# A Mamba, adapter and expert kernel: half of the scanned states leave PSUM through ScalarE and are summed by accumulating turns on TensorE, and the loop over blocks is written out

## What is computed

```
xz = hidden @ in_proj_w.T;  x, z = split(xz)              # 1024 channels each
xc = silu(causal conv over 4 tokens of x)
dt_r, Bc, Cc = split(xc @ x_proj_w.T)                     # 128, 16 and 16 columns
delta = softplus(dt_r @ dt_proj_w.T + dt_proj_bias)
def step(h, inp):                                         # h: 1024 channels x 16 states
    delta_t, B_t, C_t, x_t = inp
    dA = jnp.exp(delta_t[..., None] * A)
    h = h * dA + (delta_t * x_t)[..., None] * B_t[:, None, :]
    y_t = jnp.einsum('bdn,bn->bd', h, C_t)                # sum over the 16 states
    return (h, y_t)
y = (y + xc * D_param) * silu(z);  out = y @ out_proj_w.T
```

## Time and profile before

| what | value |
|---|---|
| median of 3 runs | 2280.05 us (2276.32 to 2281.9) |
| the profiled execution's own time | 2278.81 us |
| its span in the profile | 2276.7 us, mean granted TensorE clock 0.886 |
| busy over the span | PE 1808.2 (79%), PEld 1315.3 (58%), DVE 1619.5 (71%), ACT 791.7 (35%), POOL 1060.2 (47%) us |
| Mamba stage in the profile | scans from 132.0 to 1255.5 us, four blocks, each 283.3 us from one block's first scan to the next (699.00 to 982.28) |
| after it | adapter and expert stages up to the end |

### The profile page before, as it was taken

The page is one execution under the profiler, slowest core; times in us unless marked ns, Lnnn a source line. Parts: engine busy times, 40 slices in busy tenths (PEclk is TensorE's granted clock), DMA queues, the critical chain, the costliest instruction groups (busy, mean ns, idle before and its releaser), DMA issues. The chain is left out here.

```text
span 2276.7 us, 31205 instructions
## 1 busy us (share of the span) xinstructions
PE 1808.2 (79%) x8084; PEld 1315.3 (58%) x8084; DVE 1619.5 (71%) x2168; ACT 791.7 (35%) x1172; POOL 1060.2 (47%) x793
## 2 busy tenths in 40 slices
PE   3778767687676875768857659799988999999988
PEld 3345434454344543445534336577877888888887
DVE  0379989999899998999989354355735555555554
ACT  0444555445554445544455012210002222222222
POOL 1157557676576755767557050000005444444443
PEclk9988889788797978978879779899998999999999
DMA  5112111121011210112101142311025655565653
GB/s 137 61 33 72 38 28 34 39 72 38 28 34 39 72 40 26 34 42 69 42 24 38 61 159 81 134 56 56 21 84 115 152 134 122 145 149 115 149 143 65
DMA packets 81603, 169.61 MB, mean 74 GB/s; under 512 B 22459, under 2 KB 27467, under 8 KB 77979
## 3 DMA queue, kind: packets, MB, share of 16 engines
q1 hardware_dynamic: 57360, 116.06, 15.6%
q0 software_dynamic: 17856, 44.85, 10.2%
q10 hardware_dynamic: 6187, 6.37, 1.1%
HBM read 261.62 MB, written 39.24 MB: 132 GB/s over the span
## 5 line engine op out<-in xcount | busy, mean ns | idle before, releaser
L789 POOL TENSOR_TENSOR dbx<-u,b_all 128x512 f32<-128x512 f32 x512 | 641.5, 1276 | 354.8 <-DVE h L687 349.8
L687 DVE TENSOR_TENSOR_SCAN h<-da,dbx 128x512 f32<-128x512 f32 x512 | 596.1, 1202 | 44.5 <-ACT da L587 44.5
L587 ACT ACTIVATE da<-delta,a_neg 128x504 f32<-128x504 f32 x512 | 347.8, 684 | 469.7 <-DVE h L687 460.7
L427 PE MATMUL hT<-ident,h 128*128 128x128 f32 x2048 | 314.3, 313 | 224.5 <-DVE h L687 224.1
L427 PEld LDWEIGHTS hT<-ident,h 128*128 128x128 f32 x2048 | 274.9, 163 | 338.0 <-issue 331.3
L700 DVE SCALAR_TENSOR_TENSOR yacc<-hT,c_now,yacc 128x512 f32<-128x512 f32 x480 | 331.1, 731 | 4.3 <-PE hT L427 4.2
L334 PE MATMUL bank<-hid,w_in 128*128 128x512 f32 x608 | 290.7, 626 | 7.6 <-ACT hid L467 7.6
L1919 POOL DMA_INDIRECT out<-y,slots_kept x76 | 140.1, 1844 | 132.0 <-DMA slots_kept<-lists_kept 60.6
L334 PEld LDWEIGHTS bank<-hid,w_in 128*128 128x128 f32 x608 | 120.6, 208 | 136.3 <-issue 127.6
L1554 POOL DMA_DIRECT2D slots_kept<-lists_kept x1 | 0.6, 577 | 335.5 <-DVE lists_kept L1508 335.5
L1906 POOL DMA_INDIRECT xg_kept<-x_scratch,slots_kept x72 | 71.2, 988 | 173.8 <-issue 170.0
(11 more groups left out here) (235 smaller groups left out, 3413.5 us busy)
## 6 DMA issues: line engine op xcount, KB each, us to landing
w_up_kept<-in_up_T SPq DMA_DIRECT2D x76, 1408.0 KB, 6.2
w_dn_kept<-in_dn_T SPq DMA_DIRECT2D x76, 768.0 KB, 7.5
b_all<-bt_scratch SPq DMA_DIRECT2D x128, 256.0 KB, 3.2
x_in<-in_x_pad ACTq DMA_DIRECT2D x21, 256.0 KB
res<-in_x_pad SPq DMA_DIRECT2D x20, 256.0 KB, 3.5
x_scratch<-res SPq DMA_DIRECT2D x20, 256.0 KB, 3.4
w_in<-in_in_T SPq DMA_DIRECT2D x8, 512.0 KB, 5.0
x_in<-x_scratch SPq DMA_DIRECT2D x4, 1024.0 KB, 5.3
```

The lines of the kernel that those rows point to most:

```text
L427: mm = nc.tensor.transpose(hT[t][:, d * P:(d + 1) * P], h[:, m % RING, d, t * P:(t + 1) * P], ident[:])
L587: nc.scalar.activation(out[:, :, 1:], rows[:, :, 1:], ACT.Exp, scale=a_neg[:, d, n:n + 1]) \
L687: nc.vector.tensor_tensor_scan(h[:, n % RING, i, :], da[i % RING][:], dbx[:, i, :], 0.0, ALU.mult, ALU.add).then_inc(scan_done, 1)
L789: nc.gpsimd.tensor_tensor(dbx[:, i, :], u[:, d, :], b_all[:, m % RING, :], ALU.mult) \
```

## The change

The token tiles of a step are split between two ways. Tiles 2 and 3 (t >= BY_ACT) go on as before, through VectorE, but share one PSUM tile `hT_dve`. Tiles 0 and 1 are turned into one PSUM tile `hT_act`; ScalarE writes C times it to SBUF (`scaled`, into `hc`), and TensorE turns `hc` back with 4 transposes that accumulate in two PSUM banks `ysum` over the 16 states (`sum_up`). The four banks of hT before make room for `hT_act`, `hT_dve` and the two of `ysum`. The turn of `yacc` has half the transposes (2 uses instead of 4), VectorE adds `ysum` to `skip` apart (`add_summed`), and the gates of half 1 are two of twice the width (`gate_half`). The loop over the blocks becomes Python's, so that each engine's code is written out four times.

The order on the engines moves too. `turn_h` is now called for one tile at a time, in the order 2, 0, 1, 3. `sum_up` of tile 1 runs one step later. `first_of(m)` names the piece that stands in the middle of the step, behind the turns of tiles 2 and 0, and the rest of the pieces stand at its end. ScalarE's `scaled` stands behind decay 2 of the next step (tile 0) and behind decay 0 of the step after that (tile 1). VectorE has one `add_state` behind scan 1 and one behind scan 3 (in the first step of a half behind scan 0 and scan 1).

```diff
+def first_of(m):
+    mine = [piece for piece in LINE[m] if name_and_number(piece)[0] in EMPTIED_BY_ACT | EMPTIED_BY_DVE - {"turn"}]
+    return mine[:1] if m % NST < NST - 1 else []
...
     da = [ps(f"da{i}", [P, BLK]) for i in range(RING)]
-    hT = [ps(f"hT{t}", [P, HT * P]) for t in range(TB)]
+    hT_act = ps("hT_act", [P, HT * P])
+    hT_dve = ps("hT_dve", [P, HT * P])
+    ysum = [ps(f"ysum{q}", [P, 2, BY_ACT * P]) for q in range(PAIRS)]
...
+            def turn_h(M, t):
+                pe.wait_ge(scan_done, SCAN0 + HT * (M + 1))
+                if t < BY_ACT:
+                    pe.wait_ge(hc_made, BY_ACT * M + t)
+                    bank, full = hT_act, hT_act_full
+                else:
+                    pe.wait_ge(sum_done, BY_DVE * M + t - BY_ACT)
+                    bank, full = hT_dve, hT_dve_full
+                for d in range(HT):
+                    mm = nc.tensor.transpose(bank[:, d * P:(d + 1) * P], h[:, M % RING, d, t * P:(t + 1) * P], ident[:])
+                mm.then_inc(full, 1)
+
+            def sum_up(M, t):
+                n = M % NST
+                pe.wait_ge(hc_made, BY_ACT * M + t + 1)
...
+                for d in range(HT):
+                    mm = nc.tensor.matmul(ysum[d // 2][:, d % 2, t * P:(t + 1) * P], hc[:, t, d * P:(d + 1) * P], ident[:],
+                                          start=(n == 0 and t == 0 and d % 2 == 0), stop=(n == NST - 1), is_transpose=True, skip_group_check=True)
+                mm.then_inc(ysum_step, 1)
...
-            with pe.Fori(0, NBLK) as j:
+            for j in range(NBLK):
                 for m in range(STEPS):
-                    for piece in mine[:1]:
+                    first = first_of(m)
+                    if n == 0:
+                        piece_of("body", j, mine.pop(0))
+                    turn_h(M, 2)
+                    turn_h(M, 0)
+                    if n == 1:
+                        sum_up(M - 1, 0)
+                    if M:
+                        sum_up(M - 1, 1)
+                    for piece in first:
                         piece_of("body", j, piece)
-                    turn_h(j, m, range(0, TB // 2))
-                    for piece in mine[1:]:
+                    turn_h(M, 1)
+                    turn_h(M, 3)
+                    if n:
+                        sum_up(M, 0)
+                    for piece in mine[len(first):]:
                         piece_of("body", j, piece)
-                    turn_h(j, m, range(TB // 2, TB))
...
+            def scaled(M, t):
+                act.wait_ge(hT_act_full, BY_ACT * M + t + 1)
+                if M:
+                    act.wait_ge(ysum_step, BY_ACT * (M - 1) + t + 1)
...
+                nc.scalar.mul(hc[:, t, :], hT_act[:], c_all[:, j % RING, t, n:n + 1]).then_inc(hc_made, 1)
...
                     for i in range(HT):
                         decay(j, *divmod(m, NST), i)
+                        if i == 0 and M >= 2:
+                            scaled(M - 2, 1)
+                        if i == 2 and M:
+                            scaled(M - 1, 0)
                         if m and i % RING == RING - 1:
                             mine = [piece for piece in LINE[m - 1] if name_and_number(piece)[0] not in EMPTIED_BY_DVE | {"gate"}]
-                            for piece in (mine[:1] if i == RING - 1 else mine[1:]):
+                            first = [piece for piece in mine if piece in first_of(m - 1)]
+                            for piece in (first if i == RING - 1 else [piece for piece in mine if piece not in first]):
                                 piece_of("body", j, piece)
```

More of the change, by code:

```diff
@@ L37 @@
 SCANS = STEPS * HT
-SUMS = STEPS * TB
+ALL_STEPS = NBLK * STEPS
 RING = 2
+PAIRS = HT // 2
+BY_ACT = 2
+BY_DVE = TB - BY_ACT
 BESIDE = [
@@ L100, in uses_of @@
         of[piece] = []
-        for _ in range(HT if name == "turn" else 1):
+        for _ in range(PAIRS if name == "turn" else 1):
             uses.append(Use(uses, name in EMPTIED_BY_ACT))
@@ L243, in mamba, with c_ready @@
     x1_rows = x1_d.rearrange("(k t p) f -> k t p f", t=TB, p=P)
+    def c_ready(j):
+        return (Place("body", j - 1, "ct") if j else Place("ahead", 0, "ct")).dve + 1
     with nc.Block() as block:
@@ L374, in dt_proj, with turn @@
                     .then_inc(bank_full, 1)
-            def turn(at, half):
-                pe.wait_ge(sum_done, at.block * SUMS + SUM0 + (0 if half else SUMS // HALVES))
-                for d in range(HT):
-                    bank = take(at, d)
-                    for t in range(TB):
-                        mm = nc.tensor.transpose(bank[:, t * P:(t + 1) * P], yacc[:, t, d * P:(d + 1) * P], ident[:])
+            def turn(at, M):
+                pe.wait_ge(sum_done, BY_DVE * M)
+                for q in range(PAIRS):
+                    bank = take(at, q)
+                    for i in range(2):
+                        for t in range(BY_DVE):
+                            d = 2 * q + i
+                            mm = nc.tensor.transpose(bank[:, (i * BY_DVE + t) * P:(i * BY_DVE + t + 1) * P],
+                                                     yacc[:, t, d * P:(d + 1) * P], ident[:])
                     mm.then_inc(bank_full, 1)
@@ L647, in make_u, with add_turned, add_summed, gate_half @@
                 nc.vector.tensor_tensor(u[:, d, :], delta[:, d, :], xc[:, d, :], ALU.mult).then_inc(u_ready, 1)
[L649 to L654 removed]
+            def add_turned(at, half, q):
+                d = half * HT + 2 * q
+                dve.wait_ge(skip_ready, at.block * DT + (0 if half else d + 2) + SKIP0)
+                dve.wait_ge(bank_full, at.full + q + 1)
+                mine = skip[:, d:d + 2, BY_ACT * P:]
+                nc.vector.tensor_tensor(mine, banks[at.uses[q].bank][:].rearrange("p (i c) -> p i c", i=2), mine, ALU.add) \
+                    .then_inc(dve_emptied, 1)
+            def add_summed(M, half, q):
+                d = half * HT + 2 * q
+                dve.wait_ge(ysum_step, BY_ACT * M)
+                mine = skip[:, d:d + 2, 0:BY_ACT * P]
+                nc.vector.tensor_tensor(mine, ysum[q][:], mine, ALU.add).then_inc(ysum_out, 1)
+            def gate_half(at, M, q):
+                d = HT + 2 * q
+                dve.wait_ge(zs_ready, at.block + Z0)
+                dve.wait_ge(dve_emptied, at.dve + q + 1)
+                dve.wait_ge(ysum_out, PAIRS * (M // NST - 1) + q + 1 if M else 0)
+                nc.vector.tensor_tensor(skip[:, d:d + 2, :], skip[:, d:d + 2, :], zs[:, d:d + 2, :], ALU.mult) \
+                    .then_inc(y_ready[1], 2)
+            def finish_half(section, j, M):
+                half = 0 if M % STEPS else 1
+                at = Place(section, j, f"turn{half}")
+                if M:
+                    for q in range(PAIRS):
+                        add_summed(M, half, q)
                 if half:
[L657 to L659 removed]
+                    for q in range(PAIRS):
+                        gate_half(at, M, q)
             def residual(at, j, t):
@@ L745, in _ @@
                                 make_u(Place("body", j, piece), name_and_number(piece)[1])
-                    if n == NST - 1:
-                        for t in range(TB):
-                            add_state(j, g, n, t)
                 for piece in LINE[STEPS - 2]:
@@ L751, in _ @@
                         make_u(Place("body", j, piece), name_and_number(piece)[1])
-            for i in range(HT):
-                add_skip(Place("after", NBLK, "turn1"), 1, i)
+            for t in range(BY_DVE):
+                add_state(ALL_STEPS - 1, t)
+            for q in range(PAIRS):
+                add_turned(Place("after", NBLK, "turn1"), 1, q)
+            finish_half("after", NBLK, ALL_STEPS)
             for piece in AFTER:
@@ L803, in _ @@
                 piece_of("ahead", 0, piece)
-            with pool.Fori(0, NBLK) as j:
+            for j in range(NBLK):
                 for m in range(STEPS):
```

117 lines of the change are left out of this document (63 added, 54 removed).

## The result

The kernel after the change takes 2663.3 us (median of 4 runs, 2659.4 to 2669.4) against 2278.2 us for the kernel before (median of 4, 2275.8 to 2281.9). The ratio is 1.169, 95% interval 1.166 to 1.172: it is 17% slower, 17 us under the forecast of 2680. The profiled execution took 2662.8 us and spans 2661.0.

The account below looks back on a forecast made before the run. VectorE was taken to bound the kernel before. Steps lengthened by waits add 72 us a block, 288 in all, to 2278.8, giving 2567; the clock's 112 makes the forecast 2680 us, range 2530 to 2810.

Parts of the forecast that it names:

- x steps: Steps whose first TensorE piece is x, with two ScalarE operations: 10.7 us at full clock against 9.38 before.
- The loop through D: D: end of a step's last `add_state`; TensorE's turns and first piece wait for it; z step 10.0 us against 7.1.
- Odd out steps: Steps 6, 8, 10, 12: VectorE's residual waits for the out piece behind D; 12.4 us against 8.3.
- Even out: Steps 5, 7, 9, 11: tile 3's turn behind an unread piece; 6.95 us, 11.3 in 7 and 11, 9.2 in 9.
- The late pieces: Other pieces in ten steps, behind `sum_up` of tile 0: 2.2 to 2.8 us each, or 4 to 4.4.
- silu: Step 22, ScalarE's table loads and activations: waiting of 7.5 us after the change, 5.72 before.
- Added work: Per block: 64 `scaled` on ScalarE, 42 us; accumulating transposes on TensorE, 31 us; no engine full by its own work.
- VectorE's loss of work: Two `add_state` fewer a step on VectorE: 42 us a block, 166 us over four blocks.
- The clock: TensorE's clock stays at mean 0.84, now in VectorE's path: +28 us a block, +112 in all; chance 0.60.
- The loop written out: Python loop over blocks: removes 2 to 3 us of idle time at a block's start, nothing more.
- The first rival: TensorE's clock stays full because turns fill what were gaps: 2567 us; chance 0.12.
- the second: TensorE's clock low for most of the stage, mean 0.70: +62 us a block, 2815 us; chance 0.15.

Follow-up runs that it names:

- experiment 2: Kernel after, with each step's first piece ahead of its turns again and the others in the middle: 2206.2 us, ratio 0.973 to the kernel before.
- 3: Kernel after, with ScalarE emptying the first piece's bank behind decay 3 of the next step instead of decay 1: 2479.4 us.
- 4: Kernel before, with the first piece behind the turns of tiles 0 and 1, the others at the step's end: 2443.9 us.
- experiment 5: Kernel after, with only the first pieces ahead of their turns again, the other pieces left at the step's end: 2348.2 us.
- Experiment 7: Kernel after, with three of `sum_up`'s four transposes left out from the second state on: 2664.0 us.
- experiment 10: The kernel of experiment 2, with the convolution ahead of the second `add_state` of its step: 2219.1 us.
- 8: Kernel after, with the turns of tiles 1 and 3 issued twice: 2704.2 us.
- 9: Kernel after, with the turns of tiles 1 and 3 issued three times: 2835.3 us.
- experiment 1: Kernel before, with only the loop over the four blocks written out on all five engines: 2265.4 us, ratio 0.998.
- 6: The kernel of experiment 2, with odd out pieces one step earlier and silu in ScalarE's place behind decay 1: 2210.7 us, ratio 0.971.
- 11: The kernel of experiment 2, with three of `sum_up`'s four transposes left out for every state but the first: 2205.4 us.

## Why the prediction was right

The forecast held by its mechanism, and the time came within 17 us of it. Block 3 takes 382.2 us from its first scan (887.71) to the next block's (1269.94); the sum said 355 at the full clock and 28 for the clock, 383. By the same cuts:

| part of a block | forecast, clock at full | measured |
|---|---|---|
| steps 1 to 12 | 134 | 143.4 |
| steps 13 to 20 | 90 | 99.0 |
| steps 21 to 30 | 108 | 116.4 |
| boundary | 23 | 23.5 |
| clock | 28 | in the three above: 9.4 + 9.0 + 8.4 = 26.8 |

The last line is only what the measured parts have above the sum at the full clock. It holds the clock's part together with the errors of the single terms, and these have both signs: z and x steps at the full clock took 0.6 to 0.8 us less than was put, step 9 took 5.0 us more and step 13 4.7 us more. No run separates them, so it is in part luck that 26.8 and 28 agree.

- **The loop through D.** Shown by the z step above and by experiments 2, 3 and 4: moving the pieces back gives 457 us, moving the reader 184, moving only the pieces in the kernel before costs 173. The z step was put at 10.0 and took 9.37 at the full clock. Two terms were too large. The first is 0.25 us until ScalarE starts, 0.04 by the rows. The second is decay 2, `scaled`, decay 3 and scan 3 in a row: scan 3 stands behind scan 2, not behind decay 3, so from the end of the copy to the last `add_state` it is one decay and two scans. From decay 2 (936.37) to the next D (940.06) that is 3.69 us where 3.9 was put. The shown step is the quickest of the four z steps; together with the late dt4 and dt5 they took 47.95 us (905.76 to 953.71) where 40.4 + 5.6 = 46.0 was put, at a clock between 0.83 and 1.00.
- **x steps** were put at 10.7 at the full clock and took 9.95, for the same two terms. Where the clock was low they took longer. The rows show three D in a row, since the convolution starts at D. The first of the two steps between them begins at the half clock, the second is at the full one:

```profile
1115.40 2.96 DVE L694 SCALAR_TENSOR_TENSOR xc<-xpad,ch,xc 128x512 f32<-128x512 f32 x3
...
1128.17 2.96 DVE L694 SCALAR_TENSOR_TENSOR xc<-xpad,ch,xc 128x512 f32<-128x512 f32 x3
...
1138.12 2.96 DVE L694 SCALAR_TENSOR_TENSOR xc<-xpad,ch,xc 128x512 f32<-128x512 f32 x3
```

  The first step took 12.77 us and the second 9.95. The piece took 5.16 us in the first (1118.22, clock rising within it) and 3.60 in the next, and each of the three sets ahead of it 0.9 and 0.44.
- **Odd out steps** were put at 12.4, with a wait of about 5 us at the residual: 12.24 (960.81 to 973.05), with 5.19. **Even out**: step 5 was put at 6.95 and took 7.10. Steps 7 and 11 were put at 11.3 and took 12.9 and 12.8. Step 9 was put at 9.2 and took 14.2, at a mean clock of 0.61 and with a wait of 3.72 us of the `add_state` for its turn, which was not in the sum. The four even ones together were 47.0 in place of 38.8, the clock's part included: these steps are where the sum was furthest off.
- **The late pieces** were put at 2.2 to 2.8 or 4 to 4.4 us in ten steps, which the expectation of experiment 5 made 25 to 30 us a block; that experiment shows 142 / 4 = 35, the clock's part included.
- **silu** was put at 7.5 us of waiting, measured 7.72. The wait stands at another place than before: it is scan 0 of step 23 that waits for its decay (1164.54), since silu now stands behind decay 3 of step 22.
- **Added work.** A `scaled` 0.676 us (0.687 taken); a set of four accumulating transposes 0.60 as recorded, 0.43 from start to start (0.48 taken). Experiment 7 shows that the transposes did not make the time, and experiment 2 that all of the added work together did not.
- **VectorE's loss of work** was put at 166 us. The `add_state` lost 164 (349.1 to 184.7, both forms), but VectorE only 128: its operations that read two tensors in SBUF got slower (experiment 10 shows why). In the stage the convolutions grew from 73.7 to 88.6 us, `correct` from 22.9 to 30.4, `make_u` from 28.3 to 34.9. That cost was not in the sum; in the kernel after it is hidden by the waits, in experiment 2, where VectorE lost 138 us of work, it is part of why only 64 of the 166 us came back. The greater part is 65 us more of idle time.
- **The clock** was forecast to stay as it was: 0.84 in the stage, before and after. The first rival (full clock) and the second (0.70) both fall. What the 0.84 cost in us was taken from the share of TensorE in the path, and no run measured it. The Trainium skill's rule, TensorE: Matmul & The Clock Gate, Part 4 (PE-mode transpose), that transposes do not count as activity for the clock gate, is what stood behind the second. The runs contradict it for the fp32 transposes of this kernel: 18, 24, 32 and 40 transposes a step (experiment 7, the kernel after, 8 and 9) go with 0.77, 0.84, 0.89 and 0.89.
- **The loop written out** was to take 2 to 3 us at each block's start: experiment 1 shows 5 us less in all, with an interval from 9 less to 1 more, which can't be told from nothing.

Where the gain of experiment 2 stops is told from its groups: VectorE's work fell by 138 us in the stage and its idle time grew from 51 to 116. That its remaining waits can be removed was tried twice (6 and 11) without a gain; whether another order does it is open.

## What to carry to other kernels

When work is moved to another engine, follow the order of the instructions, not the shares of busy time: a producer placed behind something that waits for the end of a step, with its reader left early in the next step, closes a loop through three engines, and that loop cost 457 us here, where the whole change without it gains 64. Move a reader with its producer, or keep both. A wait removed from a loop that has a second one nearly as long gives nothing (experiments 6 and 11), so look at what ends next before the edit.

## What the runs showed of the hardware

- Transposes hold TensorE's clock up. With 1024 more of them in the Mamba stage, and nothing else added, the clock went from 0.84 to 0.89; with 720 fewer it fell to 0.77, and removing that work gave no time back. In experiment 11 the same 720 fewer took it from 0.94 to 0.89, and the time stayed at 2205 us.
- A transpose that accumulates in PSUM takes as long as one that does not: 324 ns as recorded against 312 and 324, a set of four 0.43 to 0.44 us from start to start at the full clock.
- VectorE's operations with two tensors in SBUF and GpSimd's hold each other up, and the rows of experiment 10 fit turns of one instruction each: VectorE's runs up to 0.89 us longer (750 to 1637 ns), and GpSimd's up to 0.44 (1271 to 1715). Scans and `add_state`, which have one input in PSUM, kept 1207 and 729 ns in the same stage of experiment 2. The Trainium skill, in GPSIMD Engine Reference, Specifications, has GpSimd's SBUF interfaces shared with VectorE, with contention for VectorE's instructions with two SBUF inputs; the trace agrees with these numbers.
